# GNN kernel, edge network: ScalarE squares tanh for the slope, and VectorE's relu gate reads TensorE's sum in PSUM

## What is computed

```python
ue = (h @ W_p1.T + b_p1)[src] + (h @ W_p2.T + b_p2)[dst]
U = _mlp3(ue, U_w0, ...)        # tanh(. @ w0.T + b0), then relu(. @ w1.T + b1), then . @ w2.T + b2
E_new = segment_sum(K[src] * U, dst)
return jnp.sum(E_new)           # and jax.grad of it
```

## Time and profile before

| | |
|---|---|
| median of 3 runs | 9600.13 us (9592.98 to 9600.5) |
| the profiled execution, its own time | 9602.42 us |
| its span, first to last instruction | 9600.4 us |
| GpSimd busy | 5429.7 us, 57% of the span |
| TensorE busy | 4956.7 us, 52% |
| VectorE busy | 4621.7 us, 48% |
| ScalarE busy | 2822.2 us, 29% |
| the edge network's loop | from about 6108 to 7129 us of the span |

### The profile page before, as it was taken

One profiled execution on the slowest core, in us unless ns is written; L12 is line 12 of the kernel. 1 busy time (PEld: TensorE's weight loads), 2 busy tenths in 40 slices (PEclk: granted clock), 3 DMA queues, 4 the chain that ended last, 5 costly groups with the idle time before them and its releaser, 6 DMA issues.

```text
span 9600.4 us, 77317 instructions
## 1 busy us (share of the span) xinstructions
PE 4956.7 (52%) x27910; PEld 2738.6 (29%) x27910; DVE 4621.7 (48%) x6121; ACT 2822.2 (29%) x2192; POOL 5429.7 (57%) x5420
## 2 busy tenths in 40 slices
PE   1000008998257777765577656344430005539977
PEld 0000007887013233221222223234420003233334
DVE  5677877776000000000498930588875301529860
ACT  0111110000000000000498920366667400519840
POOL 3777767777777777777600036788877777020000
PEclk5555555555678988987798979676665557759988
DMA  8666626443598998999799988455569716938767
GB/s 184 217 216 220 220 62 148 155 146 132 205 414 362 410 366 362 415 363 415 249 282 272 288 211 322 148 205 198 200 234 376 247 49 227 377 87 288 263 212 270
DMA packets 1228866, 2404.25 MB, mean 250 GB/s; under 512 B 566568, under 2 KB 818923, under 8 KB 1197595
## 3 DMA queue, kind: packets, MB, share of 16 engines
q1 hardware_dynamic: 1022714, 2076.35, 61.0%
q0 software_dynamic: 187136, 170.29, 6.8%
q10 hardware_dynamic: 18720, 153.79, 4.0%
HBM read 1606.44 MB, written 711.62 MB: 241 GB/s over the span
## 4 chain that ended last, share of the span: by engine, by line
POOL 36%; DMA 26%; issue 12%; PE 12%; ACT 6%; ACTq 3%; DVE 3%; DVEq 1%; SPq 1%; POOLq 0%
POOL arena L483 17%; DMA arena<-cells_w 14%; POOL xd L486 9%; POOL cells_w L486 8%; DMA arena<-cells_c 8%; PE ps L696 5%; ACT arena L1006 4%; ACTq L1005 3%; ACT arena L1004 2%; PE ps L776 2%; DMA arena<-cells_turned 2%; PE ps L861 1%; DMA arena<-hot 1%; PE ps L1137 1%; PE ps L1029 1%
## 5 line engine op out<-in xcount | busy, mean ns | idle before, releaser
L696 PE MATMUL ps<-arena 128*64 128x458 f32 (+2 forms) x7252 | 1343.3, 652 | 704.0 <-DMA arena<-cells_w 702.5
L483 POOL DMA_INDIRECT arena<-t_a,arena x832 | 940.1, 1130 | 1101.7 <-DMA t_a<-arena 848.5
L1029 PE MATMUL ps<-arena 128*33 128x400 f32 x6336 | 1161.5, 521 | 313.0 <-DVE arena L1024 305.3
L486 POOL DMA_INDIRECT sorted<-arena x832 | 844.2, 1015 | 289.1 <-issue 289.1
L714 DVE COPY carry<-ps 64x128 f32<-64x128 f32 (+1 forms) x5 | 1.5, 295 | 2045.3 <-PE ps L696 2045.3
L486 POOL DMA_INDIRECT xd<-arena x832 | 832.8, 1001 | 258.0 <-issue 253.2
L486 POOL DMA_INDIRECT cells_c<-arena x832 | 810.6, 974 | 292.8 <-issue 292.8
L486 POOL DMA_INDIRECT cells_w<-arena x832 | 812.6, 977 | 276.8 <-issue 276.8
L483 POOL DMA_INDIRECT arena<-t_kv,idx x832 | 817.0, 982 | 258.7 <-issue 253.2
L696 PEld LDWEIGHTS ps<-arena 128*64 128x64 f32 (+1 forms) x7252 | 425.7, 147 | 1618.6 <-issue 851.2
L861 PE MATMUL ps<-arena 128*96 128x400 f16 x2368 | 520.2, 373 | 424.4 <-DMA arena<-cells_c 217.5
(11 more groups left out here) (530 smaller groups left out, 9154.9 us busy)
## 6 DMA issues: line engine op xcount, KB each, us to landing
arena<-cells_w SPq DMA_DIRECT2D x245, 3200.0 KB, 18.1
arena<-cells_c SPq DMA_DIRECT2D x290, 800.0 KB, 5.2
arena<-cells_turned SPq DMA_DIRECT2D x200, 800.0 KB, 8.4
cells_w<-arena SPq DMA_DIRECT2D x49, 3200.0 KB, 20.9
weighed_cells<-arena SPq DMA_DIRECT2D x68, 1600.0 KB, 14.3
arena<-weighed_cells SPq DMA_DIRECT2D x68, 1600.0 KB, 7.3
cells_c<-arena SPq DMA_DIRECT2D x50, 1600.0 KB, 5.8
cells_turned<-arena SPq DMA_DIRECT2D x100, 800.0 KB, 5.4
```

Of the source, the lines that this page charges most:

```text
L483: return pool.indirect_dma_start(dst, None, table, bass.IndirectOffsetOnAxis(ap=index, axis=0))
L486: return pool.indirect_dma_start(table, bass.IndirectOffsetOnAxis(ap=index, axis=0), source, None)
L696: mm = pe.matmul(bank[base + k][g * f:(g + 1) * f, 0:m], rows_of, tile[:, g * width + at:g * width + at + m], start=first, stop=last, skip ...
L1029: last = pe.matmul(bank[4 * h + c][64 * kind:64 * kind + 33, 0:400], own[:, t, :], moving[:, 400 * c:400 * c + 400], start=t == 0, stop=do ...
```

## The change

VectorE no longer makes the slope. ScalarE makes t*t with one Square of 2048 numbers at the end of `up_act`, written to the same `UG2[b]`. The sign moves to two other places: ScalarE's copy to `packB` is now an activation with scale -1, and L1953 adds -1 in place of +1, so that (t*t - 1) * (-d) is what (1 - t*t) * d was. The gate compares `psO[u % 2]`, TensorE's sum in PSUM, in place of `UM[b]`. Since it now reads `psO`, TensorE waits for the gate of piece v-2 (`umlp_slope`) beside relu of that piece before it writes the bank again.

```diff
             for k in range(2 * IT):
                 b = k % 2
                 slope, hb, dr = rows(UG2[b], 64), rows(UHB, 64), rows(UDR[b], 64)
-                dve.wait_ge(S["umlp_tanh"], UG * (k + 1))
-                dve.scalar_tensor_tensor(slope, rows(UT, 64), -1.0, rows(UT, 64), ALU.mult, ALU.mult)
                 for u in range(UG):
                     t = slice(8 * u, 8 * u + 8)
                     dve.wait_ge(S["umlp_relu"], UG * k + u + 1)
-                    dve.scalar_tensor_tensor(hb[:, t, :], turned(UM[b], 64)[:, t, :], 0.0, turned(UXP[b], 64)[:, t, :], ALU.is_gt,
-                                             ALU.mult).then_inc(S["umlp_slope"], 1)
+                    dve.scalar_tensor_tensor(hb[:, t, :], psO[u % 2].rearrange("p (j f) -> p j f", f=64), 0.0,
+                                             turned(UXP[b], 64)[:, t, :], ALU.is_gt, ALU.mult).then_inc(S["umlp_slope"], 1)
...
-                    last = dve.scalar_tensor_tensor(dr[:, t, :], slope[:, t, :], 1.0, DTURN[u % 2].rearrange("p (j f) -> p j f", f=64),
+                    last = dve.scalar_tensor_tensor(dr[:, t, :], slope[:, t, :], -1.0, DTURN[u % 2].rearrange("p (j f) -> p j f", f=64),
                                                     ALU.add, ALU.mult)
...
                                    psO[u % 2].rearrange("p (j f) -> p j f", f=64), ACT.Relu).then_inc(S["umlp_relu"], 1)
+                act.activation(UG2[k % 2], UT, ACT.Square)
...
-                    act.copy(packB[u % 2], psT[u % 2]).then_inc(S["umlp_turned_copied"], 1)
+                    act.activation(packB[u % 2], psT[u % 2], ACT.Copy, scale=-1.0).then_inc(S["umlp_turned_copied"], 1)
...
                     if UG * k + v >= 2:
                         pe.wait_ge(S["umlp_relu"], UG * k + v - 1)
+                        pe.wait_ge(S["umlp_slope"], UG * k + v - 1)
```

## The result

| | median | runs |
|---|---|---|
| before | 9596.56 us | 9588.96 to 9600.5, 4 runs |
| changed | 9516.41 us | 9510.85 to 9523.44, 4 runs |

The ratio is 0.9918, with a 95% interval of 0.9901 to 0.9935: 80 us less. On a later occasion the same two kernels gave 9594.2 and 9516.13, again 0.9918 (0.9902 to 0.9935). The profiled execution of the changed kernel took 9510.85 us, its span is 9509.0.

A forecast was written before the change was run, and what follows sets the result against it. GpSimd's list was taken to bound the kernel. With the loop 258 us longer, VectorE reaches L653 at 7848, GpSimd at 7771; the later counts, so 29 of GpSimd's 106 us are gained: 9571 us, range 9497 to 9612.

The forecast's parts named there:

- the slack: Before L653, where VectorE and GpSimd meet: VectorE could come 287 us later before it would set the time.
- the ring: Hand-overs in each loop step from gate 0 to L622: L622 18.4 us behind the scan's last copy, step 10.5 us longer.

The follow-up runs named there:

- e7: Changed kernel with UX turned between relu 1 and relu 2, and VectorE's copy beside relu replaced by a second product from PSUM: ratio to before 1.0457 and 1.025.
- e4: Changed kernel with seven float32 products, read by nobody, that TensorE makes while it would wait for gate 0: 9517.62 us, ratio to before 0.9923.
- e1: Changed kernel with the gate back on SBUF and TensorE's wait on `umlp_slope` out: ratio to before 1.007, and 1.0059 on another occasion.
- e2: Kernel before with the gate on PSUM and TensorE's new wait, the slope staying on VectorE: ratio to before 1.0179.
- e3: Changed kernel with ScalarE's Square moved behind the next mask: ratio to before 1.0184, and 1.0212 on another occasion.
- e5: Changed kernel with the Square made twice, one behind the other with a drain between: ratio to before 1.0209.
- b_after: The changed kernel run again without an edit, on a later occasion: 9516.13 us, ratio to before 0.9918.

## What to carry to other kernels

Before you price an edit, find the meeting points of the engines' lists and take the slack at each: here VectorE could become 206 us later and the kernel still gained, because GpSimd had been the last one and had been stopped by VectorE's operands. An operand that moves to PSUM also keeps its bank busy until the last reader is done; ask which producer waits for that bank and what is queued behind it on every engine of the ring. When such a ring has outgrown the slack, look for a piece in it that is only there by queue order (here the turn of `UX`), and move it to where its engine waits anyway. Then see that the wait is still there when another engine is late, as e7 shows.

## What the runs showed of the hardware that I had not expected

- TensorE's clock after a pause: in 23 of 25 steps of e4 the first group of products met 1.2 GHz though TensorE had worked at 2.4 GHz until 2.3 to 2.6 us before. In the two others, with 2.64 and 2.20 us of idle time, the bias behind the pause still ran at the high clock, so the length of the pause alone doesn't decide it. The second group, with 1.11 us of idle time before it, ran at 2.4 GHz in most steps. The price of either level for a group of four products: 1.91 to 2.08 us against 1.05 to 1.16.
- How VectorE stops an indirect DMA (loops of the two kernels): one that begins while VectorE runs instructions with both tensors in SBUF, such as slope, gates or L1931, ends 0.7 to 0.9 us behind one of them; one that begins up to 0.5 us before VectorE's copy beside relu ends 0.1 us behind the copy. Those that meet no such instruction take 0.94 to 1.1 us.
- ScalarE's turn of 4096 numbers took 7.43 us in the kernel before (mean of 21) and 7.11 in the changed one (mean of 17). Within e1 alone the same instruction (L2170) took 7.11 to 7.12 in 12 steps with at most 1 us of VectorE's both-in-SBUF work beside it, and 7.23 to 7.44 in the 14 with 3 to 5 us of it. So it goes with that work; that this is the cause was not tested by itself.
- The same program took 9594 us on one occasion and 13270 to 13600 on others, with TensorE idle for some 30 us at a time with nothing to wait for. On those the kernels with the longer ring through TensorE were 2% slower than the kernel before (e2, e3 and e5), where the changed kernel was 0.8% faster here (b_after), and e1, without the longer ring, was 0.6 to 0.7% slower. I have no trace of the kernel before from there, so what it loses less is left open.
